# GNN kernel on one core: paired MLP steps in opposite row halves of TensorE, evenly split index loads, halved MLP pieces

## The reference

```python
h = jnp.maximum(_layernorm(x, axis=-1), 0.0)
# layer 0: mean of the 64 edge features per target node, then an MLP
agg = segment_sum(edge_attr_64, dst, 6250) / maximum(counts, 1)
combined = concatenate([agg, h], axis=1)            # 6250 x (64 + 256)
x = x + relu(combined @ W1 + b1) @ W2 + b2          # 320 -> 512 -> 256
h = jnp.maximum(_layernorm(x, axis=-1), 0.0)
# layer 1: mean of the neighbours' rows
x = x + h @ w_self.T + b_self + (segment_sum(h[src], dst, 6250) / maximum(deg, 1)) @ w_neigh.T
```

## Time and profile before

| | |
|---|---|
| runs, us | 1209.31, 1209.85, 1210.40 (median 1209.85) |
| the profiled execution | 1212.18 us, its span 1210.4 us |
| granted TensorE clock, mean | 0.978 |
| busy share | PE 93%, PEld 71%, DVE 67%, ACT 43%, POOL 35% |
| edge groups begin and end | 28.6 us and about 357 us |
| MLP steps 7 to 12 | about 370 to 481 us |
| dense layer 1 | from about 495 us |

### The profile page before, as it was taken

How to read it: one execution, slowest core, us unless ns; L and a number is a source line. 1 busy time by engine, 2 the same in 40 slices (tenths; PEclk the granted TensorE clock), 3 DMA queues, 4 the chain that set the end, 5 groups by cost and what they waited for, 6 DMA issues and landing times.

```text
span 1210.4 us, 31419 instructions
## 1 busy us (share of the span) xinstructions
PE 1120.6 (93%) x11712; PEld 864.0 (71%) x11712; DVE 805.9 (67%) x1812; ACT 520.0 (43%) x987; POOL 419.7 (35%) x384
## 2 busy tenths in 40 slices
PE   1789999999988989799999999999999999999996
PEld 1678788787777877577677777767767777776774
DVE  3777778777862467766666666766667666676661
ACT  2555635333111446444444444544444444454441
POOL 3011111110004650436354444534635444453361
PEclk9999999999997999799999999999999999999998
DMA  6766545545561210212121121211212112121121
GB/s 183 251 208 202 189 151 163 160 152 159 167 202 43 81 42 27 61 54 79 50 75 58 54 67 59 69 56 52 74 52 74 55 52 69 59 70 57 53 75 34
DMA packets 67057, 116.15 MB, mean 96 GB/s; under 512 B 10645, under 2 KB 30825, under 8 KB 66963
## 3 DMA queue, kind: packets, MB, share of 16 engines
q1 hardware_dynamic: 51922, 75.12, 19.7%
q0 software_dynamic: 15040, 39.80, 11.8%
HBM read 101.93 MB, written 12.95 MB: 95 GB/s over the span
## 4 chain that ended last, share of the span: by engine, by line
PE 81%; DVE 7%; issue 4%; DVEq 3%; DMA 2%; ACT 2%; another core or an unknown queue 1%; ACTq 0%; SPq 0%
PE bank L1163 35%; PE couples L1156 10%; PE couples L992 9%; PE bank L1182 7%; PE bank L961 6%; PE bank L951 5%; PE bank L949 3%; PE couples L997 2%; PE bank L1174 2%; PE bank L1194 1%; DMA hreg<-in_dst_dram 1%; PE couples L918 1%; DMA kreg<-in_edge_attr_dram 1%; DVE oreg L1604 1%
## 5 line engine op out<-in xcount | busy, mean ns | idle before, releaser
L1163 PE MATMUL bank<-hreg,areg 128*128 128x512 f16 x2058 | 504.7, 382 | 0.0
L596 POOL DMA_INDIRECT wide<-h_table,aggn x280 | 324.0, 1157 | 414.8 <-PE couples L1156 194.7
L806 ACT ACTIVATE areg<-couples 128x784 bf16<-128x784 f32 x336 | 276.7, 824 | 369.7 <-PE couples L1156 362.9
L1163 PEld LDWEIGHTS bank<-hreg,areg 128*128 128x128 bf16 x2058 | 265.7, 144 | 104.5 <-issue 1.1
L1604 DVE TENSOR_TENSOR hids<-iota,kreg 128x1024 bf16<-128x1024 f16 x336 | 196.5, 626 | 49.9 <-PE couples L1156 48.6
L1604 DVE TENSOR_TENSOR oreg<-iota,kreg 128x1024 bf16<-128x1024 f16 x336 | 195.8, 624 | 44.7 <-PE couples L1156 43.2
L992 PE MATMUL couples<-oreg,kreg 128*64 128x48 f32 x3232 | 138.6, 230 | 30.8 <-DVE oreg L1356 15.7
L992 PEld LDWEIGHTS couples<-oreg,kreg 128*64 128x64 f32 x3232 | 119.2, 142 | 59.5 <-issue 55.1
L1356 DVE TENSOR_TENSOR oreg<-iota,wide 128x384 f32<-128x384 f32 x202 | 116.5, 578 | 4.3 <-issue 1.1
L1156 PEld LDWEIGHTS couples<-oreg 128*128 128x128 bf16 x1344 | 76.8, 98 | 49.3 <-issue 13.7
L563 POOL TENSOR_TENSOR xr<-xr,b2bc 128x512 f32 x25 | 33.7, 1350 | 223.6 <-ACT h0buf L686 223.6
(11 more groups left out here) (164 smaller groups left out, 1063.3 us busy)
## 6 DMA issues: line engine op xcount, KB each, us to landing
kreg<-in_edge_attr_dram SPq DMA_DIRECT2D x202, 256.0 KB, 2.8
h_table<-hreg SPq DMA_DIRECT2D x25, 256.0 KB
xr<-in_x_dram SPq DMA_DIRECT2D x6, 1024.0 KB, 7.1
out_dram<-hbuf SPq DMA_DIRECT2D x42, 128.0 KB
wide<-h_table,aggn POOLq DMA_INDIRECT x280
wide<-in_L_gnn_W_dram SPq DMA_DIRECT2D x2, 512.0 KB, 5.5
out_dram<-h0buf SPq DMA_DIRECT2D x6, 128.0 KB
hreg<-in_dst_dram SPq DMA_DIRECT2D x1, 512.0 KB
```

What stands on the lines that cost most here:

```text
L596: pool.indirect_dma_start(near[:, k, :], None, table, bass.IndirectOffsetOnAxis(ap=nearsrc[:, n * GHALF + k:n * GHALF + k + 1], axis=0)).t ...
L806: act.activation(step.rearrange("p (a k) -> p a k", a=2), cpl[s % 2][:, :, 0:BC * KEYS], ACT.Copy).then_inc(s_adj, 1)
L1163: ins = pe.matmul(bank[4 + par], adj[:, par, :, h], htab[:, h, :], start=(h == 0), stop=(h == TN - 1))
```

## The change

1. The 73-row index DMA is split in one of 64 rows and one of 9; the waits on it count four DMAs.
2. The two `base` loads go. TensorE transposes column 0 of the index table instead, into one row of a PSUM bank, and VectorE copies that row to `base`.
3. `AHEAD` is 2: part 2 of `x` is no longer loaded in front, and parts 2 to 5 are loaded behind every third set of six edge loads, not every fourth.
4. The edge means of q = 1 are written to partitions 64 to 127, and `w1a` holds the 64 weight rows twice. The matmuls of q = 0 and q = 1 with the edge means use 64 rows each, one behind the other, in different PSUM banks. The zero rows and their two memsets go; SyncE's wait for GpSimd is for one memset.
5. `hidden` is now a piece for one (k, b, q): with q = 0 it issues both edge-mean matmuls and its own two of the node part, with q = 1 only the two of the node part. `outer` is cut in two matmuls. Sixteen pieces stand behind groups 0, 1, 3, 4, 6, 7, ... 21, 22.
6. ScalarE's `hidden` goes by k, for both q; step 12 uses the 64-row form for its one q.

```diff
-    AHEAD = 3
+    AHEAD = 2
+    EVEN = 64
...
+        def hidden_bank(q, k, own):
+
+            return bank[(4 + q, 4 + q - 2 * k, 4 + k)[own]]
...
-            sp.dma_start(into[0:G1 - 1, 1, :], v[G0 * GE:GF * GE].rearrange("(g j) -> g j", g=G1 - 1)).then_inc(done, 16)
+            for lo, hi in ((0, EVEN), (EVEN, G1 - 1)):
+                sp.dma_start(into[lo:hi, 1, :], v[(G0 + lo) * GE:(G0 + hi) * GE].rearrange("(g j) -> g j", g=hi - lo)
+                             ).then_inc(done, 16)
...
-            with nc.allow_non_contiguous_dma(reason="one index of each group"):
-                sp.dma_start(base[0:1, 0:GF], dst[0:GF * GE].rearrange("(g j) -> j g", g=GF)[0:1, :]).then_inc(s_base, 16)
-            sp.dma_start(base[0:1, GF:G], dst[E - GE:E - GE + 1].rearrange("(a b) -> a b", a=1)).then_inc(s_base, 16)
...
-                sp.dma_start(w1a[0:FE, :], w1[0:FE, :]).then_inc(s_w, 16)
+                for q in range(2):
+                    sp.dma_start(w1a[q * FE:(q + 1) * FE, :], w1[0:FE, :]).then_inc(s_w, 16)
...
-            sp.wait_ge(s_zero, 2)
+            sp.wait_ge(s_zero, 1)
...
                 for part in range(AHEAD, XPARTS):
-                    for i in range(SPAN):
-                        load_slots(SPAN * (part - AHEAD) + i + 1)
+                    for i in range(SPAN - 1):
+                        load_slots((SPAN - 1) * (part - AHEAD) + i + 1)
                     load_x(part)
...
-            pool.memset(w1a[:, :], 0.0).then_inc(s_zero, 1)
...
-            pool.memset(aggn[:, :, :], 0.0)
...
-            def hidden(i, q, own=0):
-
-                if later(i):
-                    act.wait_ge(s_outp[q], i)
-                for k in range(2):
+            def hidden(i, k, own=0):
+
+                for q in range(1 if own == 2 else 2):
+                    if k == 0 and later(i):
+                        act.wait_ge(s_outp[q], i)
                     act.wait_ge(s_hidp[q], 2 * i + k + 1)
...
+            for b, m in ((0, G0), (1, G1)):
+                ins = pe.transpose(bank[6][0:1, b * P:b * P + m], raw[0:m, b, 0:1], ident[0:m, 0:m])
+            ins.then_inc(s_basep, 1)
...
+            def hidden(i, k, b, q, own=0):
+
+                cols = slice((2 * k + b) * P, (2 * k + b + 1) * P)
+                if q == 0:
+                    qs = range(1 if own == 2 else 2)
+                    for e in qs:
+                        if b == 0:
+                            if k == 0:
+                                if not later(i):
+                                    pe.wait_ge(s_const, 2)
+                                pe.wait_ge(s_agg[e], i + 1)
+                            if own or k == 1 or later(i):
+                                pe.wait_ge(s_hids[e], 2 * i + (k - (own > 0)))
+
+                    for e in qs:
+                        pe.matmul(hidden_bank(e, k, own)[:, b * NM:(b + 1) * NM], w1a[e * FE:(e + 1) * FE, cols],
+                                  aggn[e * FE:(e + 1) * FE, e, :], start=True, stop=False)
+                    if k == 0 and b == 0:
+                        pe.wait_ge(s_h0T, 2 * i + len(qs))
...
+                for h in range(DH):
+                    ins = pe.matmul(hidden_bank(q, k, own)[:, b * NM:(b + 1) * NM], w1b[:, h, cols],
+                                    h0T[:, bass.ds(2 * u, 2), h, :], start=False, stop=(h == DH - 1))
+                if b == 1:
+                    ins.then_inc(s_hidp[q], 1)
...
-                for b in range(HB):
+                for b in range(half * HB // 2, (half + 1) * HB // 2):
...
+            pieces = [(hidden, k, b, q) for k in range(2) for b in range(2) for q in range(2)]
+            pieces += [(outer, q, t, half) for q in range(2) for t in range(2) for half in range(2)]
+            parts = {3 * (n // 2) + n % 2: piece for n, piece in enumerate(pieces)}
...
-                for q in range(2):
-                    for k in range(2):
-                        hidden(i, q, k, own=1)
-                outer(i, 0, 0)
-                outer(i, 0, 1)
+                all_hidden(i)
+                all_outer(i, 0)
...
-            hidden(U // 2, 0, 0, own=1)
-            hidden(U // 2, 0, 1, own=1)
+            all_hidden(U // 2, own=2)
...
+            dve.wait_ge(s_basep, 1)
+            dve.tensor_copy(base[0:1, :], bank[6][0:1, 0:G]).then_inc(s_base, 1)
...
-                dve.tensor_tensor(aggn[0:FE, q, :], acc[0:FE, bass.ds((2 * i + q) * NM, NM)], deg[:, :],
+                dve.tensor_tensor(aggn[q * FE:(q + 1) * FE, q, :], acc[0:FE, bass.ds((2 * i + q) * NM, NM)], deg[:, :],
```

More of the change, by code:

```diff
@@ L777, in layer0 @@
             def layer0(i, n=None):
-                hidden(i, 0)
+                hidden(i, 0, own=1)
                 hidden(i, 1, own=1)
@@ L792, in _ @@
                 layer0(KEY0 + n, n)
-            hidden(U // 2 - 1, 0)
+            hidden(U // 2 - 1, 0, own=1)
             hidden(U // 2 - 1, 1, own=1)
@@ L798, in _ @@
             copy_places(2)
-            hidden(U // 2, 0)
+            hidden(U // 2, 0, own=2)
+            hidden(U // 2, 1, own=2)
             def copy_counts(t, par, s):
@@ L957, in outer @@
+            def outer(i, q, t, half):
+                if t == 0 and half == 0:
                     if later(i):
@@ L959, in outer, with all_hidden, all_outer @@
                     pe.wait_ge(s_hids[q], 2 * i + 2)
-                for b in range(HB):
+                for b in range(half * HB // 2, (half + 1) * HB // 2):
                     ins = pe.matmul(bank[6 + q][:, t * D:(t + 1) * D], hids[:, q, b, t * P:(t + 1) * P], w2s[:, b, :],
                                     start=(b == 0), stop=(b == HB - 1))
-                if t == 1:
+                if t == 1 and half == 1:
                     ins.then_inc(s_outp[q], 1)
+            def all_hidden(i, own=1):
+                for k in range(2):
+                    for b in range(2):
+                        for q in range(1 if own == 2 else 2):
+                            hidden(i, k, b, q, own)
+            def all_outer(i, q):
+                for t in range(2):
+                    for half in range(2):
+                        outer(i, q, t, half)
+            pieces = [(hidden, k, b, q) for k in range(2) for b in range(2) for q in range(2)]
+            pieces += [(outer, q, t, half) for q in range(2) for t in range(2) for half in range(2)]
+            parts = {3 * (n // 2) + n % 2: piece for n, piece in enumerate(pieces)}
             def counts_by_node(t0, t1):
@@ L978, in complete_counts @@
                 counts_by_node(0, 4 * (BESIDE + 1))
-            parts = {0: (hidden, 0, 0), 3: (hidden, 0, 1), 6: (hidden, 1, 0), 9: (hidden, 1, 1),
-                     12: (outer, 0, 0), 15: (outer, 0, 1), 18: (outer, 1, 0), 21: (outer, 1, 1)}
             with pe.If(in_windows(pe)):
@@ L1024, in span @@
                         if i is not None and j in parts:
-                            part, a, b = parts[j]
-                            part(i, a, b)
+                            part, *which = parts[j]
+                            part(i, *which)
                         if j % SLOTS == SLOTS - 1 and j // SLOTS < pairs:
@@ L1060, in _ @@
                 loop(pe, any_group, 1, G)
-                pe.wait_ge(s_w, 8 * 16)
+                pe.wait_ge(s_w, 9 * 16)
                 def any_layer0(i):
-                    for part, a, b in parts.values():
-                        part(i, a, b)
+                    for part, *which in parts.values():
+                        part(i, *which)
                 any_layer0(0)
@@ L1202, in _ @@
                 if s == 1:
-                    outer(U // 2, 0, 0)
-                    outer(U // 2, 0, 1)
+                    all_outer(U // 2, 0)
                     near_transposes()
@@ L1440, in mean_by @@
                 dve.wait_ge(s_hidp[q], 2 * i)
-                dve.tensor_tensor(aggn[0:FE, q, :], acc[0:FE, (2 * i + q) * NM:(2 * i + q + 1) * NM],
+                dve.tensor_tensor(aggn[q * FE:(q + 1) * FE, q, :], acc[0:FE, (2 * i + q) * NM:(2 * i + q + 1) * NM],
                                   bank[0][0:FE, q * NM:(q + 1) * NM], ALU.mult).then_inc(s_agg[q], 1)
```

46 lines of the change are left out of this document (13 added, 33 removed).

## The result

The changed kernel takes 1202.70 us (four runs, 1200.63 to 1204.04), the kernel before 1209.63 us beside it: a ratio of 0.994, 95% interval 0.9923 to 0.9957, so 6.9 us less. The forecast was 1195 us, 14.6 us less. The sign is right and the time lies in the range, but less than half of the gain is there. The profiled execution took 1202.83 us, its span 1200.9 us.

The account below looks back on a forecast made before the run. TensorE was taken as the bound, with 81% of the chain of waits. Front -13.5, spans -2, steps 7 and 8 -0.8, step 12 +1.0 made -15.3 on 1212.2 us: 1196.9, or about 1195 as median; range 1185 to 1204.

Parts of the forecast that it names:

- Index load and `base`: Front: index table there at about 6 us, -12.0 us (-9 to -13.5); copy of `base` on VectorE +0.3, later `x` +0.5.
- the 21 that the prediction itself had set as the sign of being wrong: Front: first one-hot expected at about 17 us; the prediction is wrong if it comes after 21 us.
- Fewer `x` loads: Front: TensorE's wait for edges, 2.3 us in one piece, taken as gone, -2.3 us (0 to -4).
- Spans: Seven spans of edge groups with MLP pieces: -0.3 us each, -2 us in all.
- The pair: Spans: edge-mean matmuls of both halves run side by side in four pairs, -1.73 us a span (bounds nothing and 1.73).
- Eight more pieces: Spans: eight added switches between column-half groups and full-width matmuls at 0.28 us each, +2.24 us a span.
- Stalls: Spans: 1.4 of TensorE's 2.2 us of waits a span gone (0 to 2.2), as pieces separate the groups.
- the one wait at step 10: Spans: new wait of VectorE at its step 10 for the q = 0 means, behind group 9's hidden piece; called just covered.
- A: Rival, spans dearer: pairs hardly overlap or switches cost full drains, 0.9 to 1.4 us a span, 1201 to 1205 us; chance 0.17.
- B: Rival, spans cheaper: all stalls go and extra switches hide behind VectorE's pace, -1 us more a span, 1188 us; chance 0.14.
- Steps 7 to 12: MLP steps without edge groups: steps 7 and 8 -0.8 us, steps 9 to 11 0, step 12 +1.0 us (0 to 1.2).
- `outer(0)` now follows right behind the last hidden matmuls: MLP steps without groups: ScalarE's two relus against 0.86 us of q = 1 matmuls, 0.2 us lost.

Follow-up runs that it names:

- version with both repairs: Changed kernel with GpSimd's `acc` memset behind VectorE's casts and steps 7 to 12 in the form of before: 1187.66 us, ratio 0.9806; again 1186.95 us, 0.9805.
- the square above: Span times of four versions: whole pieces 40.12 us over 128 rows, 39.77 in pairs; halved pieces 40.18 over 128 rows, 39.25 in pairs.
- the front alone: Kernel before with points 1 to 3 of the change and nothing of the MLP: 1203.22 us, ratio 0.9945.
- control: Changed kernel unaltered, run again on another occasion: 1193.33 us, ratio 0.9853.

## Why the prediction was right and wrong

**Index load and `base`: the load right, the sum wrong.** The table was there at 6.18 us (forecast 6). The base copy takes 0.35 us, but costs nothing: from table to first one-hot it is 10.67 us with the memset moved and 10.66 before, since the copy lies in a wait for the range check. The step that failed is the sentence "Nothing else holds the chain so early: the memset of `acc` ends at 11.1 us, the first one-hot is due at about 17". It asked who waits for the memset, and not what VectorE does while it runs. The earlier trace rows had both numbers: casts from 6 us would lie in a memset from 5.66 to 11.09. That cost 4.3 us, and 21.15 us for the first one-hot is behind the 21 that the prediction itself had set as the sign of being wrong. With the memset moved, the first one-hot is at 17.38 us, as forecast, and group 36 at 64.95, 12.9 us earlier than before against the 13.5 forecast; in the three other versions with the memset moved it is at 66.45 to 67.74, 10.1 to 11.4 us earlier.

**Fewer `x` loads: right in part.** Groups 0 to 11 took 13.9 us (up to 14.7 in other versions) and not 15.5; TensorE's wait for edges went from 2.3 us to 0.7. Groups 12 to 35 took 35.4 us and not 33.7, at a mean clock of 0.81 instead of 0.90. The kernel with the memset moved took 33.7 for them at a mean clock of 0.85, the version with both repairs, the same there, 36.5 at 0.77 in its second profile. So this stretch moves by up to 2.8 us between profiles that differ in nothing there, and 35.4 is the middle of the 19 profiles with the new front: some 1.7 us of the front's gain go here, against the one profile of before, and I didn't follow why.

**Spans: 0.87 us gained and not 0.3.** By its terms:
- The pair. It saves 0.43 us against the same rows in turn (1.06 to 0.63), as written. But the kernel before didn't pay 1.06; it paid 0.86 for two matmuls over 128 rows. "4 x 0.43 = 1.73 us go" less 0.56 for switches makes 1.17; the square above has 40.18 - 39.25 = 0.93, which is 4 x 0.23.
- "Eight more pieces: 8 x 0.28 = +2.24." This is the mis-sized term. In the row over 128 rows, halving changed the span by +0.06 while TensorE's waits fell from a mean of 1.5 to 0.4 us (the three spans of the front alone wait 1.2, 2.2 and 1.2): 1.2 us for eight pieces, 0.15 each. In pairs it is -0.52 with 1.5 us of waits gone, 0.12 each. 0.28 was read from two pieces of the old form; a further piece costs half of that.
- Stalls: 1.4 forecast, 1.1 to 1.5 measured. Right, with the reason given: nothing but the one wait at step 10 is left.

The rivals A and B were both about this sum. B's direction was right, its 1 us a span was not reached. The measured 1202.7 us lies in A's range, 1201 to 1205, but by luck: the pairs overlap in full, and the spans came out cheaper, not dearer.

**Steps 7 to 12: +0.2 forecast.** Undisturbed (control against the front alone) it is 102.6 - 100.7 = +1.9 us. "4 x 0.43 - 4 x 0.28 = 0.6 saved" fails for the same reason as above: step 8 takes 17.97 us, with 128 rows 17.71, so nothing is saved. Steps 11 and 12 together, to the couples, came out 1.5 us dearer (25.86 against 24.35) where 1.0 was forecast for step 12. The loop over outer, layer norm and keys in steps 9 to 11 is as forecast when undisturbed.
Disturbed, it is up to +12.0 us. The sentence that failed is "`outer(0)` now follows right behind the last hidden matmuls: ScalarE's two relus against 0.86 us of matmuls of q = 1, 0.2 lost". The price is right for signals in time: 0.8 us of waits in the control's five steps. But it took every signal for prompt. The trace of before had a pair 3.9 us late (423.5 us), and the old order, with the two hidden parts of q = 1 between the relus of q = 0 and their use, let TensorE pass over such signals: in the seven profiles with that order it waited for relus once, 0.35 us, apart from the 1.8 us that I put in by mistake. A cover of 2.6 us went for a gain of 0.6, and I asked only what it hides in the ordinary case. The pairing is not to blame for the waits: with the new order over 128 rows they are there too, 5.2 us. The old order is no shield against everything: the kernel before lost 4.7 us in its step 9 (24.2 against 19.5), with its wait for the keys, and what led to that wasn't followed.

**The whole.** Three comparisons of the changed kernel gave 0.994, 0.9853 and 0.9902. The second, without late pairs in its profile, is 1191.8 us on the 1209.6 of before, within 3.2 us of the forecast. But that is two errors that cancel (front 6.1 us short, spans 6.4 us over), with the disturbed tail absent. Where the forecast comes out, it isn't for its reasons.

**What stays open.** Why TensorE's signals come late wasn't found. That the stores aren't needed is shown by holding them back. That it has to do with GpSimd's gathers rests on 21 of 27 late pairs just ahead of a resumption; that the gathers are the cause, and that their phase decides, is argued and not shown, since the unaltered kernel is with and without late pairs by itself. That it takes a run of more than two gathers rests on one profile. The half-clock stretches aren't settled either: of the 14 waits of 2.3 us or more of TensorE for relus or keys in all these tails 10 had one right behind, and four hadn't (3.18 us, the longest of those).

## What to carry to other kernels

Before pulling a stage forward, lay its instructions over what the other engines do at the new time: here a cast met a memset that it had always missed, and a wait of GpSimd for the right signal gave 4.3 us back. An order that keeps independent work between a result and its use is worth more than its mean wait shows; look through the trace for the latest signals it covers before giving it up for a few tenths. And price a shared half by what the kernel pays now, not by the same half used twice.

## What the runs showed of the hardware

- Matmuls in opposite 64-row halves run together: records 7 ns apart, 0.63 us for a pair of float32 matmuls of 256 columns, 1.06 us in the same half one behind the other, 0.86 us over all rows. A lone visit to 64 rows between 128-row matmuls costs 0.39 us.
- VectorE's cast from int32 to float32 stands still while GpSimd's memset runs (5.61 us for 1.29), a reduction doesn't (1.22 us).
- Signals of TensorE reached VectorE and ScalarE up to 3.9 us behind their matmuls in steps where GpSimd issued gathers one behind the other, two of them then together, while TensorE's own work went on if it needed none of them. The cause is open.
- With lone half-row matmuls the granted clock stayed at the lower level for 37.5 us (346.4 to 383.9, one profile), 29 us of them after step 7 had begun, though TensorE was busy for 32.0 of the 37.5. In the version with both repairs it rose after 13.7 us, 5 us into step 7, and in the changed kernel 3.6 us into it. This cost about 11 us of step 7's 34.5 (an estimate: 34.5 less the 20.2 of the version with both repairs and 3.1 for eight visits).
